# Gate and up weights of an SwiGLU block loaded as one joined transfer instead of two

## The reference

```python
xn = layernorm(x)
# branch s: a linear recurrence along the sequence
u  = xn @ W_in.T + b_in
h_t = exp(lambda_log) * h_{t-1} + gamma * u_t
s  = h @ W_out.T + b_out + xn
# branch g: a SwiGLU block with integer weights, hidden size 3072
g  = silu( (silu(xn @ wg.T) * (xn @ wu.T)) @ wd.T )    # wg, wu, wd = w_int / 127
out = x + s * g
```

## Time and profile before

| | us |
|---|---|
| runs of the kernel | 1400.13 and 1628.44 (median 1514.29) |
| the profiled execution | 1391.55 |
| its span on the slowest core (core 6) | 1390.0 |
| its spans on all 8 cores | 1369.6 to 1390.0 |
| TensorE busy, core 6 | 1300.8 (94%) |
| TensorE's mean granted clock, all cores | 0.986 to 0.994 |

### The profile page before, as it was taken

How to read it: one execution, slowest core, us unless ns; L and a number is a source line. 1 busy time by engine, 2 the same in 40 slices (tenths; PEclk the granted TensorE clock), 3 DMA queues, 4 the chain that set the end, 5 groups by cost and what they waited for, 6 DMA issues and landing times.

```text
span 1390.0 us, 15972 instructions; the slowest of 8 cores (1369.6 to 1390.0 us)
## 1 busy us (share of the span) xinstructions
PE 1300.8 (94%) x6032; PEld 589.3 (42%) x6032; DVE 350.2 (25%) x566; ACT 289.9 (21%) x437; POOL 198.1 (14%) x197
## 2 busy tenths in 40 slices
PE   0799999999997999989999899999999899999997
PEld 0444345444453434534454344544445344454443
DVE  1323320334012240123301233022320323113232
ACT  2521123110231102311222112221123110231100
POOL 1000031300321003300043000330021300221002
PEclk9999999999998999999999999999999999999999
DMA  9955406753077520675126651376405753066401
GB/s 194 258 155 152 121 17 195 221 150 86 31 226 197 139 73 31 233 219 151 33 77 235 177 149 30 132 233 170 131 16 197 213 149 94 31 204 185 127 1 61
DMA packets 224622, 190.91 MB, mean 137 GB/s; under 512 B 5027, under 2 KB 201763, under 8 KB 224548
## 3 DMA queue, kind: packets, MB, share of 16 engines
q1 hardware_dynamic: 201364, 103.91, 27.9%
q0 software_dynamic: 23184, 85.99, 19.1%
HBM read 177.29 MB, written 16.78 MB: 140 GB/s over the span
## 4 chain that ended last, share of the span: by engine, by line
PE 85%; DMA 11%; issue 1%; DVE 1%; SPq 1%; ACT 0%; DVEq 0%; ACTq 0%; POOL 0%; POOLq 0%
PE pb L342 24%; PE pb L296 21%; PE pb L304 20%; DMA wubuf<-wu_t 9%; PE pb L273 9%; PE pb L324 8%; PE pb L254 2%; DMA xbuf<-xe 2%; PE pb L319 1%; SPq L515 0%; DVE stats L196 0%; DVE hbT L467 0%; SPq L158 0%; ACT xnb L235 0%; DVE xbuf L495 0%
## 5 line engine op out<-in xcount | busy, mean ns | idle before, releaser
L296 PE MATMUL pb<-xnbT,wgbuf 128*128 128x512 bf16 x1536 | 369.7, 385 | 39.2 <-DMA wubuf<-wu_t 31.5
L304 PE MATMUL pb<-xnbT,wubuf 128*128 128x512 bf16 x1536 | 366.1, 382 | 0.0
L342 PE MATMUL pb<-wdfull,hbT 128*128 128x512 bf16 x1536 | 332.8, 379 | 0.0
L467 DVE SCALAR_TENSOR_TENSOR hbT<-pb,siluT 128x512 bf16<-128x512 f32 x192 | 132.8, 692 | 615.4 <-PE pb L304 615.4
L296 PEld LDWEIGHTS pb<-xnbT,wgbuf 128*128 128x128 bf16 x1536 | 148.9, 98 | 231.9 <-issue 61.4
L399 ACT ACTIVATE siluT<-pb 128x512 bf16<-128x512 f32 x192 | 114.6, 597 | 587.9 <-PE pb L296 584.8
L304 PEld LDWEIGHTS pb<-xnbT,wubuf 128*128 128x128 bf16 x1536 | 151.1, 98 | 185.5 <-issue 6.9
L342 PEld LDWEIGHTS pb<-wdfull,hbT 128*128 128x128 bf16 x1536 | 150.0, 98 | 181.6
L539 POOL TENSOR_TENSOR gslab<-gslab,s_sb 128x512 bf16<-128x512 bf16 x60 | 71.4, 1189 | 858.4 <-ACT gslab L357 851.3
L273 PE MATMUL pb<-xnbT,winT 128*128 128x512 bf16 (+1 forms) x576 | 122.3, 375 | 4.4 <-ACT guT L388 4.4
L324 PE MATMUL pb<-woutT,guT 128*128 128x512 bf16 x512 | 121.6, 381 | 0.0
(11 more groups left out here) (29 smaller groups left out, 242.6 us busy)
## 6 DMA issues: line engine op xcount, KB each, us to landing
wgbuf<-wg_t SPq DMA_DIRECT2D x96, 512.0 KB, 4.3
wubuf<-wu_t SPq DMA_DIRECT2D x96, 512.0 KB, 6.1
wdfull<-wd_t POOLq DMA_DIRECT2D x32, 1536.0 KB, 15.2
out<-xbuf POOLq DMA_DIRECT2D x32, 512.0 KB, 3.1
xbuf<-xe POOLq DMA_DIRECT2D x7, 2048.0 KB, 11.1
winT<-win_t POOLq DMA_DIRECT2D x1, 2048.0 KB, 25.8
xbuf<-xe SPq DMA_DIRECT2D x1, 2048.0 KB, 24.5
woutT<-wout_t POOLq DMA_DIRECT2D x1, 2048.0 KB, 21.1
```

Of the source, the lines that this page charges most:

```text
L296: O("tensor", lambda eng, g=g, cc=cc, kc=kc, gb=gb: eng.matmul(pb[gb][:, 0:512], wgbuf[g % 2][:, kc * 256 + cc * 128: kc * 256 + cc * 128 ...
L304: O("tensor", lambda eng, g=g, cc=cc, kc=kc, ub=ub: eng.matmul(pb[ub][:, 0:512], wubuf[g % 2][:, kc * 256 + cc * 128: kc * 256 + cc * 128 ...
L342: O("tensor", lambda eng, c=c, m=m, n=n: eng.matmul(pb[2 * m + n][:, 0:512], hbT[:, c * T + m * 128: c * T + m * 128 + 128], wdfull[:, c * ...
L467: O("vector", lambda eng, c=c: eng.scalar_tensor_tensor(hbT[:, c * T:(c + 1) * T], pb[3 + 2 * (c % 2)][:, 0:512], QINV, siluT[c % 2][:, :] ...
```

## The change

The two weight tensors in HBM become one, `wgu_t` [1024, 6144]: for each group, its 256 gate columns and then its 256 up columns lie side by side. The two pairs of buffers become one pair, `wgubuf[i]`, of the same total size. For each group SyncE issues one DMA of 1 MB in rows of 1024 bytes instead of two of 512 KB in rows of 512 bytes. The matmuls read the same values at other offsets. The semaphore now rises by 16 for each group and not by 32. The order of the work, the waits, and all other engines' instructions stay as they are. The joining is done on the host, outside the device time.

```diff
-    wg_t = di("wg_t", [D, H], BF16)
-    wu_t = di("wu_t", [D, H], BF16)
+    wgu_t = di("wgu_t", [D, 2 * H], BF16)
...
-    wgbuf = [sb(f"wgbuf{i}", [128, NK * 256], BF16) for i in range(2)]
-    wubuf = [sb(f"wubuf{i}", [128, NK * 256], BF16) for i in range(2)]
+    wgubuf = [sb(f"wgubuf{i}", [128, NK * 512], BF16) for i in range(2)]
...
-                            wgbuf[g % 2][:, kc * 256 + cc * 128: kc * 256 + cc * 128 + 128],
+                            wgubuf[g % 2][:, kc * 512 + cc * 128: kc * 512 + cc * 128 + 128],
...
-                            wubuf[g % 2][:, kc * 256 + cc * 128: kc * 256 + cc * 128 + 128],
+                            wgubuf[g % 2][:, kc * 512 + 256 + cc * 128: kc * 512 + 256 + cc * 128 + 128],
...
-                for wi, (wsrc, wdst) in enumerate(((wg_t, wgbuf),
-                                                    (wu_t, wubuf))):
-                    src = wsrc[:, g * 256:(g + 1) * 256].rearrange(
-                        "(kc p) h -> p kc h", p=128)
-                    dst = wdst[g % 2][:, :].rearrange("p (kc h) -> p kc h", h=256)
-                    O("sync", lambda eng, s=src, d=dst: eng.dma_start(d, s),
-                      inc=f"s_wgu{G % 2}", n=16,
-                      mark=None if wi == 0 else ("wgu", G))
+                src = wgu_t[:, g * 512:(g + 1) * 512].rearrange(
+                    "(kc p) h -> p kc h", p=128)
+                dst = wgubuf[G % 2][:, :].rearrange("p (kc h) -> p kc h", h=512)
+                O("sync", lambda eng, s=src, d=dst: eng.dma_start(d, s),
+                  inc=f"s_wgu{G % 2}", n=16, mark=("wgu", G))
```

More of the change, by code:

```diff
@@ L632, in make_in_maps @@
         "wout_t": np.ascontiguousarray(w_out.T),
-        "wg_t": np.ascontiguousarray(wg.T).astype(bf),
-        "wu_t": np.ascontiguousarray(wu.T).astype(bf),
+        "wgu_t": np.ascontiguousarray(np.concatenate(
+            [np.ascontiguousarray(wg.T).reshape(D, NGU, 256),
+             np.ascontiguousarray(wu.T).reshape(D, NGU, 256)],
+            axis=2).reshape(D, 2 * H)).astype(bf),
         "wd_t": np.ascontiguousarray(wd.T).astype(bf),
```

## The result

| | before | after |
|---|---|---|
| runs, median us (number) | 1396.5 (10) | 1375.49 (11) |
| ratio of after to before | | 0.9844, 95% interval 0.9809 to 0.9879 |
| the profiled execution | 1391.55 | 1373.18 |
| span of the slowest core | 1390.0 (core 6) | 1371.7 (core 1) |
| span, mean of the 8 cores | 1382.9 | 1359.7 |

The kernel is 1.6% faster, some 22 us (means of 1394.6 and 1372.9 us). The medians of all tables are of every run, a few of which ran with the cores of one die or of both at a lower clock, and the ratios, like the two means, leave those out. Ten runs of before, taken in two sessions, have their median at 1396.5, between the profiled execution and the run of 1400.13 that stood beside it when the prediction was made.

The account below looks back on a forecast made before the run. Late gate/up loads, at the edge of one group's time, and the clock dips behind them cost TensorE time. Waits 13.9 us plus clock 2.3 made 16 us, off the profiled 1391.55: 1376 us, range 1354 to 1398.

Parts of the forecast that it names:

- The bound and the edge: Gate/up stages: 25 of 96 groups start 37.8 us late in all; in time if the second DMA takes under 6.15 us.
- The row size: Gate/up load: 64 packets of 1 KB at 53 ns replace 128 of 512 bytes, saving 0.4 us of engine time.
- The joined DMA: Gate/up load: one DMA instead of two saves 0.2 us of fixed cost per landing.
- The sum: TensorE's gate/up waits: 0.6 us saved per landing gives 13.9 us, with 2.3 us for the clock 16 us in total.
- the clock: Slower matmuls after gate/up waits: half of the 4.5 us behind waits of 2.0 to 2.5 us goes, 2.3 us.
- the equal saving for every wait: Late gate/up groups: each longer wait loses 0.6 us, also beside the x load; waits of 0.32 to 0.64 vanish nearly whole.
- B: Rival on gate/up loads: each DMA has a full fixed cost, about 2 us saved per landing, 1351 us; chance 0.17.
- C: Rival on gate/up loads: landing doesn't move, savings of 0 to 0.2 us, 1387 to 1392 us; chance 0.21.
- D: Rival on gate/up loads: the joined load lands later, each 0.1 us costing 4.8 us of kernel; chance 0.06.
- The signs named beforehand: Profile after: quiet landing about 5.2 us, median 5.9, packets 50 to 56 ns, 15 to 20 waits totalling 20 to 25 us.

Follow-up runs that it names:

- ring4_4k_x_later: Kernel before with four one-chunk gate/up buffers, one DMA per chunk in 4 KB rows, and the x load held back to the S stage: 1336.83 us, ratio 0.9639.
- rows_256: Kernel before with gate/up weight rows of 256 bytes instead of 512, still two DMAs per group: 1431.45 us, ratio 1.0346.
- one_dma_512: Changed kernel with rows of 512 bytes as before, still one DMA of 1 MB per group: 1379.92 us, ratio to the kernel before 0.9962.
- before_x_later: Kernel before with only GpSimd's load of x held back to the S stage: 1356.54 us, ratio 0.9778.
- x_load_later: Changed kernel with GpSimd's load of x held back to the S stage: 1343.87 us, ratio to the kernel before 0.9736.
- two_dmas_1k: Changed kernel with each group's load again two DMAs of 512 KB, rows kept at 1 KB: 1375.9 us, ratio to the kernel before 0.9937.

## Why the prediction was right, point by point

**The bound and the edge: right.** TensorE had 34.3 us of waits per core at the first gate matmul, and from there the time came: 17.0 us of waits and the 6.0 us of slower matmuls behind them. The waits "for VectorE" were the load's: they vanished when the loads came in time, in ring4_4k_x_later. rows_256 showed the edge from its other side.

**The row size: right in kind, the term too small.** 53 ns was forecast for a 1 KB packet, 52.5 came. (The packets taken for 4 KB have 3946 bytes as their mean, 6.20 MB / 1571 in the earlier trace rows; with that the line gives 55 ns, which changes little.) But the 512-byte packet, taken at 29.6 ns from a quiet stretch, costs 30.8 over the execution, as the earlier trace rows had said with 31.3. So a load's engine time fell by (6205 - 5333) / (96 x 16) = 0.57 us, not 0.4. The landing in quiet fell by 0.6 us for the rows with two DMAs, but by 0.35 with one.

**The joined DMA: right in size of order.** 0.2 forecast; in quiet one_dma_512 shows 0.3 in one stretch and 0.4 over all its quiet loads. The two terms were added, 0.2 + 0.4; in the runs they overlap, and together they gave 0.7 us for the 0.6 of the forecast.

**The sum: both terms low, the clock's by more than half.** 13.9 us of waits forecast, 17.0 came as the mean of the cores; 2.3 us for the clock forecast, 6.0 came. The second was cautious by choice, half of 4.5 us, with the two longest waits kept whole. In fact the longest waits shrank too: 5.1 to 6.7 us on each core before, 2.2 to 4.9 on seven of eight after. As the mean of the cores, the longest fell from 6.0 to 3.6 us, by 2.4 where 0.6 was forecast. The step at fault is the equal saving for every wait; the landing, 0.7 instead of 0.6 us, adds a little. The prediction had seen that beside the x load a doubled packet moves twice the bytes in a turn, put the gain there between 0.4 and 1.4 us, and took 0.6 like elsewhere. before_x_later and x_load_later say that less than half of the change's worth is left once the x load is out of the way (6.7 of 17.0 us of waits, 10.3 of 23.2 us of mean span). That engines share by turns of packets, the reason which the prediction gave for this, no run shows.

**The predicted time, 1376, and the measured, 1375.49:** two errors that offset each other, and so the nearness is luck. The gain was 22 us and not 16, and the base was 1396.5 and not the 1391.55 of the profiled execution. As a ratio the forecast was 1376 / 1391.55 = 0.9888, just outside the measured interval of 0.9809 to 0.9879. Between the two profiled executions the gain was 18.4 us, since core 1 kept 25.3 us of waits.

**The rivals.** B, the full fixed cost of a DMA, fell with one_dma_512: half the DMAs with the old rows left 24.8 of 34.3 us of waits. The fit of the Trainium skill that the prediction put beside B (DMA: Bandwidth & Descriptors, "Anatomy of one DMA") is stated there for DMAs that GpSimd issues; these are SyncE's. C, no effect of the packet size, fell with the share of q1 and with two_dmas_1k; the rule of the Trainium skill (same page, "Specifications"), by which rows of 512 bytes are at line rate, is not borne out here: the engines need 16% more time for them than for 1 KB (6205 against 5333 engine-us; 30.8 x 2 against 52.5 is 17%), and 8 KB are faster still. The 3 cycles a packet of the Trainium skill (same page, "Why small descriptors are slow (HBM only)") have the right direction; the 8% between the two sizes that the prediction estimated from them are about half of what q1 shows. D fell: in quiet the joined load lands earlier.

**The signs named beforehand:** quiet landing about 5.2 us (5.3), packets of 50 to 56 ns (52.5), 15 to 20 places with 20 to 25 us (core 1: 18 with 25.3), waits of 4 to 5 us beside the x load still there (4.87 and 3.86). The median landing of 5.9 was met by no core: 5.2 to 5.6 on six, 6.3 and 6.4 on two.

**What stays open:** why on one or two cores, not always the same, the loads land 0.5 to 1 us later than on the others. The traffic of other cores on the same HBM is a possible reason; no run here tests it.

## What to carry to other kernels

Where a double-buffered load is allowed the time of one stage and takes nearly that, work out the edge first (stage time less issue and wake-up, here 6.15 us against a median landing of 6.1), since there 0.1 us of landing was worth about 3 us of kernel when it was saved and 5 us when it was lost. Longer contiguous rows and one DMA for two halves that are awaited together are cheap to have, but look also at what runs beside the late loads: moving one unhurried 2 MB load out of the stage gained more (0.9778), and cutting the buffers finer, with the same memory and rows of 4 KB, more again (0.9706; with rows of 512 bytes only 0.9837). Take a wait's saving at its place and not as a mean, the longest above all, because it is mostly behind those that the matmuls are slow (3.57 us for 1.89 after waits of 5.3 us in the earlier trace rows and after the 3.9 us wait of core 1).

## What the runs showed of the hardware

- A packet's engine time is a line in its bytes from 261 bytes to 1 KB: 8.8 ns + 0.043 ns a byte (19.9, 30.8, 52.5 ns), and near it at 6.7 KB (313 ns, 295 by the line). No step shows at 512 bytes. All four are means over q1 of a whole execution.
- Two DMAs issued 0.41 us apart on one queue landed only 0.4 us later than one of the same bytes and 512-byte rows (medians of 6.0 and 5.6 us in quiet).
- Beside a load of x of 2 MB, a gate/up load of 1 MB landed 11.35 us after its issue on core 1, against 5.3 in quiet.
